# Reordering the front of a fused two-layer kernel: norm powers, table load, modulation and one gating product

## The chip, the cores and the metric

The kernel runs on one core of a Trainium2 chip. A core has five engines that run side by side and meet only at semaphores: TensorE (PE, matrix products; PEld is its weight load), VectorE (DVE), ScalarE (ACT), GpSimd (POOL) and SyncE (SP, which here only issues DMAs). The metric is the device time of one execution in microseconds (us). Three runs of the kernel before gave 589.02, 590.26 and 590.35 us, median 590.26 us.

## The reference

Two residual layers work on x of shape 2 x 1024 x 128 (2048 tokens). Each layer has a mixer half and a feed-forward half, and each half has a LayerNorm, a modulation by a condition vector c (scale `ca`, shift `sa`) and a gate `ga`:

```python
mod = (_silu(L0_c) @ L0_wmod).reshape(L0_c.shape[0], 6, 1, -1)
sa, ca, ga, sb, cb, gb = (mod[:, 0], mod[:, 1], mod[:, 2], mod[:, 3], mod[:, 4], mod[:, 5])
h = _layernorm(x, axis=-1) * (1 + ca) + sa
x = x + ga * _L0_attn_ref(h, ...)
h = _layernorm(x, axis=-1) * (1 + cb) + sb
x = x + gb * _L0_ffn_ref(h, ...)
```

The change is in the first half of layer 0, the spiking mixer `_L0_attn_ref`:

```python
r = jax.nn.sigmoid(jnp.einsum('btd,ed->bte', x, W_r) + b_r)
ek = jnp.exp(jnp.einsum('btd,ed->bte', x, W_k) + b_k)
v = jnp.einsum('btd,ed->bte', x, W_v) + b_v
td = jnp.exp(b_td)
g = jnp.exp(global_decay)
def step(carry, inputs):
    sa, sb, mem = carry
    ek_t, v_t, r_t = inputs
    sa = ek_t * v_t + td * sa
    sb = ek_t + td * sb
    wkv = (g * ek_t * v_t + sa) / (g * ek_t + sb + EPS)
    inp_t = r_t * wkv
    reset = spike_fn(mem - THRESH)
    mem = BETA * mem + inp_t - reset * THRESH
    spk = spike_fn(mem - THRESH)
    return ((sa, sb, mem), spk)
```

After it come two layers of windowed attention with rotary positions and a gelu MLP (layer 0's feed-forward half), a complex linear recurrence (layer 1's mixer), and a mixture of a shared and eight routed experts. The change does not touch them.

## The kernel before

Everything is written as one hand-ordered instruction list per engine; no scheduler reorders it. What an engine issues next is what stands next in its function, and an instruction that waits for a semaphore holds back everything behind it on the same engine.

The tokens are cut into NG = 4 groups of 512 (a group is 4 tiles of 128 tokens). For the mixer the work on a group g goes round all engines:

- DVE computes the LayerNorm statistics of the group's four tiles (`mixer_stats(g)`, L837 to L843) and signals `ln_var`. From the third group on, `ln_stats(n)` first waits until `ln_norm` has reached 4*(n-1), that is, until ACT has normalised group n-2, because the two halves of the statistics buffer are reused.
- POOL raises the variance to the power -1/2 and multiplies by the negated mean (`ln_rstd`, L610 and L611), which signals `ln_rstd`.
- ACT normalises token-major (`mixer_norm(g)`, L359, four instructions, signals `ln_norm`). PE transposes the result (`ln_t2`, L1297). ACT applies modulation scale and shift while it copies it out of the accumulator (`mixer_out(g)`, L365, into `hsA`); for group 0 it first waits for `mod_fin`, the modulation vector from PE (L1336) and DVE (L859 to L867). ACT also copies the transposed input (`mixer_x(g)`, L373).
- PE multiplies by the key weights (L1350) and the value weights (L1353). ACT takes the exponential (L394), scales it (L397, signals `ek_ready`) and makes the denominator's first part `gek` (L399).
- DVE multiplies key by value (L883), scans twice (L889 and L891), forms the numerator (L894, signals `num_ready`) and takes the reciprocal (L897) of the denominator, to which POOL added the scan (L662).
- The quotient and the gating by the sigmoid `rsg` are products of 128 x 512 elements. For groups 0 to 2 POOL does them (`quotient` L651, `current` L657); for group 3 DVE does both (L923, L925).

ACT computes the sigmoids after its loop over the groups. It needs a table of coefficients per set of functions; `load_table` is a tiny instruction that pulls the load to a chosen place. At the start POOL also raises e to the decays and to other per-channel vectors (L631 to L643; `sc_ready` tells that those which ACT needs at L397 are there).

When the gated currents of all groups are there, DVE runs the membrane recurrence as PASSES = 4 passes over chunks of 16 steps (L913 and L917, all 64 chunks of a sequence side by side). The fourth pass checks that the states at the chunks' starts no longer change; if they do, a further checked pass runs. Then the spikes are added to x, and the second norm, the attention and all else follow. PE has products of the identity with itself (`warm`, L1329) before and after the modulation, and after it waits for each group's normalised input in turn.

Of the kernel before, what the change touches and what calls it, by code (L numbers as in the profile page):

```python
# [16 lines left out]
P = 128  # L17
# [58 lines left out]
def program(nc, a, out):  # L76
    with ExitStack() as ctx:
# [266 lines left out]
        def _(act):  # L344
# [23 lines left out]
            def mixer_norm(g):  # L368
                ln_norm(ln_no(0, g), xt[:, g * TPG:(g + 1) * TPG, :])

            def mixer_x(g):
                act.wait_ge(s["xT_fill"], g + 1)
                act.activation(x_cm[:, gsl(g)], psT0[:, :], ACT.Copy).then_inc(s["xT_evac"], 1)  # L373

            def load_table(function):

                act.activation(sc[:, 9:10], half[:, 0:1], function).then_inc(s["table"], 1)
# [6 lines left out]

            mixer_norm(0)
            mixer_x(0)
            mixer_norm(1)
            act.wait_ge(s["init"], 2)
            load_table(ACT.Exp)
            mixer_out(0)  # L390
            for g in range(NG):

                act.wait_ge(s["kv_mm"], 2 * g + 1)
                own.one(act.activation(ek[:, gsl(g)], psS[:, g % 2, :], ACT.Exp, bias=vec[:, V_BK:V_BK + 1]))  # L394
                if g == 0:
                    act.wait_ge(s["sc_ready"], 1)
                act.activation(ek[:, gsl(g)], ek[:, gsl(g)], ACT.Identity, bias=0.0, scale=sc[:, 1:2]).then_inc(s["ek_ready"], 1)  # L397
                act.wait_ge(s["ek_ready"], g + 1)
                act.activation(gek[:, gsl(g)], ek[:, gsl(g)], ACT.Identity, bias=sc[:, 3:4], scale=sc[:, 2:3]).then_inc(s["gek_ready"], 1)  # L399
                if g + 1 < NG:  # L400
                    mixer_x(g + 1)
                    mixer_out(g + 1)
                if g + 2 < NG:
                    mixer_norm(g + 2)
# [191 lines left out]
        def _(pool):  # L596
# [32 lines left out]

            pool.wait_ge(s["ld_c"], 32)  # L630
# [6 lines left out]
            ln_rstd(ln_no(0, 0))  # L637
            ln_rstd(ln_no(0, 1))
# [34 lines left out]
            current(2)  # L673

# [155 lines left out]
        def _(dve):  # L830
# [91 lines left out]
            dve.wait_ge(s["num_ready"], NG)  # L922
            own.one(dve.tensor_tensor(ekv[:, c], ekv[:, c], gek[:, c], ALU.mult))  # L923
            dve.wait_ge(s["r_ready"], NG)
            own.one(dve.tensor_tensor(ekv[:, c], ekv[:, c], rsg[:, c], ALU.mult))  # L925
            dve.wait_ge(s["cur_ready"], NG - 1)
# [366 lines left out]
        def _(pe):  # L1293
# [17 lines left out]

            pe.wait_ge(s["ld_c"], 32)
# [27 lines left out]
            warm(6)  # L1340
            modulation(0, psQK[:, 0, :])
            warm(4)

            ln_t2(ln_no(0, 0))
# [466 lines left out]
```

## Time and profile before

| what | value |
| --- | --- |
| median of three runs | 590.26 us (589.02 to 590.35) |
| profiled execution: its time, its span | 588.94 us, 587.0 us |
| busy share PE, DVE, ACT, POOL | 83%, 77%, 59%, 53% |
| mean granted TensorE clock | 0.929 of full speed |
| start of the stage: DVE's first product of key and value | 17.86 us |
| start of the membrane passes | 48.73 us |
| end of the four passes and their check (next DVE work) | 96.90 us |

The profile is of one execution. The span runs from its first to its last instruction; 1.94 us lie around it. The shares of busy time are means over stages with different limits, so they do not tell what bounds the mixer's front, which ends at 48.73 us. For that a reader takes the timelines of that stretch, engine by engine, and asks of each instruction whether its engine was idle before it and what released it. A timeline line is: start, duration, engine, source line, operation, written tile <- read tiles, shapes, count of merged instructions, and in brackets the idle time before it with its releaser. Instructions of an engine overlap a little, so that the next one can start before start plus duration. An fp32 product is recorded as two instructions.

### The profile page before, as it was taken

The numbers are of one execution on the slowest core, as the hardware profiler recorded it, in microseconds if no ns is written. First come the engines' busy times: TensorE is split into PE (matmuls) and PEld (weight loads), VectorE is DVE, ScalarE is ACT, GpSimd is POOL, SyncE is SP. The second block draws the span as 40 slices with busy tenths as digits, with TensorE's granted clock in tenths as the row PEclk, the third lists the DMA queues.
The fourth block names the chain that finished last, engine by engine and source line by source line (L and its number), as shares of the span: only waits on it lengthen the run. The fifth ranks groups of instructions, "written<-read, shape, count | busy, mean of one in ns | idle before, by whom it ended". The sixth has DMA issues, their size and how long they took to land. (4 is left out here: it accounts for less than half of the span.)

```text
span 587.0 us, 11694 instructions
## 1 busy us (share of the span) xinstructions
PE 488.2 (83%) x3996; PEld 310.8 (53%) x3996; DVE 452.3 (77%) x1201; ACT 348.0 (59%) x1000; POOL 308.5 (53%) x248
## 2 busy tenths in 40 slices
PE   4741004579999999899989999999899999999996
PEld 4411002336777776644347777776644445657774
DVE  5799998779899996646698999996454687457775
ACT  4870000638999998743369999997746535532332
POOL 6650000478888888855878888887001266120000
PEclk9795556689999999999999999999999999999999
DMA  8300000201111111200021111111000000000100
GB/s 302 129 2 0 1 1 1 72 19 28 39 37 39 37 39 37 73 2 1 0 73 39 37 38 38 39 38 35 13 0 2 0 1 1 1 0 5 30 22 18
DMA packets 14192, 18.87 MB, mean 32 GB/s; under 512 B 2186, under 2 KB 8628, under 8 KB 14004
## 3 DMA queue, kind: packets, MB, share of 16 engines
q1 hardware_dynamic: 13844, 18.04, 11.1%
q8 instruction: 32, 0.52, 0.4%
q14 instruction: 28, 0.23, 0.1%
q10 hardware_dynamic: 288, 0.08, 0.1%
HBM read 8.94 MB, written 1.05 MB: 17 GB/s over the span
## 5 line engine op out<-in xcount | busy, mean ns | idle before, releaser
L485 ACT ACTIVATE prob<-psS,nmx 128x128 f32<-128x128 f32 x256 | 89.9, 377 | 21.8 <-DVE nmx L1045 21.8
L610 POOL TENSOR_TENSOR rst<-mv,half 128x4 f32<-128x4 f32 x24 | 25.7, 1069 | 135.0 <-DVE mv L843 124.2
L749 POOL TENSOR_TENSOR rn<-ssq,half 128x16 f32<-128x16 f32 x32 | 93.2, 2911 | 4.3 <-DVE ssq L1031 1.3
L741 POOL TENSOR_TENSOR ra<-ra,rb 128x512 f32<-128x512 f32 x64 | 80.1, 1273 | 3.1 <-DVE rb L1013 3.1
L1371 PE MATMUL psQK<-wqkv,hsA 128*128 128x512 f32 x128 | 64.2, 627 | 2.2 <-ACT z L365 2.2
L359 ACT ACTIVATE lnx<-psT,nmr,rst 128x128 f32<-128x128 f32 x48 | 18.0, 457 | 78.1 <-POOL nmr L611 78.1
L485 ACT ACTIVATION_READ_ACCUMULATOR prob<-psS,nmx 128x1 f32 x256 | 55.5, 217 | 0.0
L757 POOL TENSOR_TENSOR qkn<-ra,rn 128x512 f32<-128x512 f32 x32 | 33.3, 1042 | 28.7 <-DVE qkn L1039 28.7
L1010 DVE TENSOR_TENSOR ra<-psQK,rope 128x512 f32<-128x512 f32 x64 | 43.9, 686 | 5.6 <-PE psQK L1371 5.1
L1013 DVE TENSOR_TENSOR rb<-psQK,rope 128x512 f32<-128x512 f32 x64 | 43.6, 681 | 0.0
L1045 DVE TENSOR_REDUCE nmx<-psS 128x4 f32<-128x512 f32 x64 | 41.1, 683 | 3.1 <-PE psS L1455 3.1
L1297 PEld LDWEIGHTS psT<-ident,qkn 128*128 128x128 f32 x256 | 30.0, 142 | 24.3 <-issue 15.3
L592 ACT ACTIVATE gel<-psQK 128x512 f32<-128x512 f32 x32 | 19.1, 597 | 39.7 <-PE psQK L1655 39.7
L1024 DVE TENSOR_REDUCE ssq<-sq 128x8 f32<-128x512 f32 x64 | 40.9, 676 | 0.2
L1377 PE MATMUL psO<-masks,identb 128*128 128x512 bf16 x12 | 4.5, 557 | 43.8 <-DVE vAB L917 43.8
L1297 PE MATMUL psT<-ident,qkn 128*128 128x128 f32 x256 | 34.5, 276 | 5.8 <-DVE qkn L1039 4.4
L459 ACT ACTIVATE pT<-psT 128x512 f32<-128x512 f32 x64 | 36.5, 656 | 3.0 <-PE psT L1297 3.0
L1473 PE MATMUL psO<-vAB,pT 128*64 128x64 f32 x1024 | 36.9, 225 | 1.6 <-ACT pT L459 1.6
L1297 PEld LDWEIGHTS psT<-ident,prob 128*128 128x128 f32 x256 | 29.7, 140 | 16.0 <-issue 14.0
L1473 PEld LDWEIGHTS psO<-vAB,pT 128*64 128x64 f32 x1024 | 32.4, 138 | 7.7 <-ACT pT L459 5.8
L1409 PE MATMUL psO<-wqkv,hsA 128*128 128x512 f32 x64 | 35.8, 642 | 0.0
L1039 DVE TENSOR_TENSOR qkn<-ra,rn 128x512 f32<-128x512 f32 x32 | 22.1, 691 | 17.7 <-POOL rn L749 17.3
(231 smaller groups left out, 1200.8 us busy)
## 6 DMA issues: line engine op xcount, KB each, us to landing
vAB<-vAB SPq DMA_DIRECT2D x62, 128.0 KB, 2.2
wqkv<-in_wqkv SPq DMA_DIRECT2D x2, 768.0 KB, 7.4
big<-in_x SPq DMA_DIRECT2D x4, 256.0 KB, 4.6
ropeb<-in_rope SPq DMA_DIRECT2D x1, 1024.0 KB, 6.5
big<-in_ew SPq DMA_DIRECT2D x2, 512.0 KB, 4.3
out<-big SPq DMA_DIRECT2D x4, 256.0 KB, 2.3
wmod<-in_wmod SPq DMA_DIRECT2D x2, 384.0 KB, 5.8
w<-in_w SPq DMA_DIRECT2D x2, 341.0 KB
```

Source lines behind the costliest of these rows:

```text
L459: act.activation(pT[:, 4 * hb:4 * hb + 4, :], four((psT0, psT1)[hb]), ACT.Copy).then_inc(s["pT_evac"], 1)
L485: act.activation(prob[:, k, :], psS[:, hb, c * P:(c + 1) * P], ACT.Exp, bias=nmx[:, k:k + 1], accum_out=sums[:, n % 2, k:k + 1]).then_inc( ...
L741: pool.tensor_tensor(o, o, rb[:, r], ALU.add).then_inc(s["sum_" + name], 1)
L749: pool.tensor_tensor(rn[:, :], ssq[:, :], half[:, :], ALU.pow).then_inc(s["rn_ready"], 1)
L1010: dve.tensor_tensor(heads(o), heads(psQK[:, part, :]), rope[:, at8, 2 * part, :].unsqueeze(1).to_broadcast([P, H, DH]), ALU.mult).then_inc ...
L1013: dve.tensor_tensor(rb[:, r].rearrange("p (h a d) -> p h a d", h=H, a=2), psQK[:, part, :].rearrange("p (h a d) -> p h a d", h=H, a=2)[:, ...
L1024: dve.tensor_reduce(ssq[:, 8 * part:8 * part + 8], heads(sq[:, part * INNER:(part + 1) * INNER]), AX.X, ALU.add).then_inc(s["ssq_" + name], 1)
L1045: dve.tensor_reduce(nmx[:, 4 * hb:4 * hb + 4], psS[:, hb, :].rearrange("p (h k) -> p h k", h=4), AX.X, ALU.max, negate=True).then_inc(s["n ...
L1297: i = pe.transpose(dst[:, k * P:(k + 1) * P], src(k), ident[:, :])
L1371: mm(psQK[:, part, :], hsA[:, tile(i)], wqkv[:, part * INNER:(part + 1) * INNER], start=True, stop=True).then_inc(s[name + "_mm"], 1)
L1409: mm(psO[:, 1, :], hsA[:, tile(i)], wqkv[:, 2 * INNER:3 * INNER], start=True, stop=True).then_inc(s["v_fill"], 1)
L1473: j = mm(psO[64 * w:64 * w + 64, 0, h * DH:(h + 1) * DH], pT[:, slot(h), 64 * w:64 * w + 64], (vA, vB)[w][:, u, h * DH:(h + 1) * DH], star ...
```

## The change

Five things move or are added, all in the mixer:

1. POOL raises the first two groups' variances (`ln_rstd` of groups 0 and 1) before the decays instead of after them.
2. ACT loads the table for Exp right after the silu of the condition, before the first norm; it waits for the first of POOL's two memsets only.
3. ACT's norm of group 1 moves from before `mixer_out(0)` to behind group 0's three key instructions; in the same way each norm of group g+1 now stands directly ahead of the copies of group g+1 instead of one group earlier. 
4. PE runs seven 128 x 128 products on zeros (the cleared `kT2`) ahead of its first wait for an input, does the modulation directly behind the first transposes, then three products of the identity, the transposes of the normalised group 0, and four more products of the identity.
5. The gating product of group 3 goes from DVE (L925) to POOL, on the numerator before the quotient: POOL waits for `num_ready` and `r_ready` of all groups and signals `cur_ready`; DVE then has one product left ahead of the passes.

```diff
--- before.py
+++ after.py
@@ -382,11 +382,10 @@
                 b = bof(g)
                 ln_out(ln_no(0, g), hsA[:, gsl(g)], mod[:, 0, CA, b:b + 1], mod[:, 0, SA, b:b + 1])
 
+            act.wait_ge(s["init"], 1)
+            load_table(ACT.Exp)
             mixer_norm(0)
             mixer_x(0)
-            mixer_norm(1)
-            act.wait_ge(s["init"], 2)
-            load_table(ACT.Exp)
             mixer_out(0)
             for g in range(NG):
 
@@ -398,10 +397,9 @@
                 act.wait_ge(s["ek_ready"], g + 1)
                 act.activation(gek[:, gsl(g)], ek[:, gsl(g)], ACT.Identity, bias=sc[:, 3:4], scale=sc[:, 2:3]).then_inc(s["gek_ready"], 1)
                 if g + 1 < NG:
+                    mixer_norm(g + 1)
                     mixer_x(g + 1)
                     mixer_out(g + 1)
-                if g + 2 < NG:
-                    mixer_norm(g + 2)
             for g in range(NG):
                 act.wait_ge(s["r_mm"], g + 1)
                 own.one(act.activation(rsg[:, gsl(g)], psQK[:, g % 2, :], ACT.Sigmoid, bias=vec[:, V_BR:V_BR + 1]))
@@ -627,6 +625,8 @@
 
 
 
+            ln_rstd(ln_no(0, 0))
+            ln_rstd(ln_no(0, 1))
             pool.wait_ge(s["ld_c"], 32)
             own.one(pool.memset(fr[:, 0:1], float(np.e)))
             own.did(pool.tensor_tensor(sc[:, 0:1], fr[:, 0:1], vec[:, V_BTD:V_BTD + 1], ALU.pow))
@@ -634,8 +634,6 @@
             own.one(pool.tensor_scalar(fr[:, 1:2], vec[:, V_BTD:V_BTD + 1], 0.0, -T / 2, ALU.max, ALU.mult))
             own.one(pool.tensor_tensor(sc[:, 1:2], fr[:, 0:1], fr[:, 1:2], ALU.pow))
             pool.tensor_scalar(sc[:, 3:4], sc[:, 1:2], 1e-6, 0.0, ALU.mult, ALU.add).then_inc(s["sc_ready"], 1)
-            ln_rstd(ln_no(0, 0))
-            ln_rstd(ln_no(0, 1))
             for dst, src in ((4, V_NU), (5, V_TH), (6, V_GAM)):
                 own.did(pool.tensor_tensor(sc[:, dst:dst + 1], fr[:, 0:1], vec[:, src:src + 1], ALU.pow))
             own.sync()
@@ -671,6 +669,9 @@
                     current(1)
                     quotient(2)
             current(2)
+            pool.wait_ge(s["num_ready"], NG)
+            pool.wait_ge(s["r_ready"], NG)
+            pool.tensor_tensor(ekv[:, gsl(3)], ekv[:, gsl(3)], rsg[:, gsl(3)], ALU.mult).then_inc(s["cur_ready"], 1)
 
             C1 = 1.0 / (2 * np.pi)
             CH = float(np.round(C1 * 4096 * 4) / (4096 * 4))
@@ -919,11 +920,8 @@
 
 
             dve.wait_ge(s["rcp_ready"], NG)
-            dve.wait_ge(s["num_ready"], NG)
+            dve.wait_ge(s["cur_ready"], NG)
             own.one(dve.tensor_tensor(ekv[:, c], ekv[:, c], gek[:, c], ALU.mult))
-            dve.wait_ge(s["r_ready"], NG)
-            own.one(dve.tensor_tensor(ekv[:, c], ekv[:, c], rsg[:, c], ALU.mult))
-            dve.wait_ge(s["cur_ready"], NG - 1)
             for _ in range(PASSES - 1):
                 membrane_pass(both)
             for st in both:
@@ -1309,6 +1307,10 @@
                 four(out_bank(n), lambda k: lnx[:, n % 2, k, :]).then_inc(s["ln_t2"], 1)
 
 
+            pe.wait_ge(s["init"], 2)
+            nought = kT2[:, 0, 0:2, :]
+            for _ in range(7):
+                mm(psO[:, 0, 0:P], nought, nought, start=True, stop=True)
             pe.wait_ge(s["ld_c"], 32)
 
             def mixer_turn(g):
@@ -1337,11 +1339,10 @@
                            silc[:, 2 * k:2 * k + 2], start=True, stop=True)
                 i.then_inc(s["mod_mm"], 1)
 
-            warm(6)
             modulation(0, psQK[:, 0, :])
+            warm(3)
+            ln_t2(ln_no(0, 0))
             warm(4)
-
-            ln_t2(ln_no(0, 0))
             pe.wait_ge(s["ld_wr"], 16)
             for g in range(NG):
                 pe.wait_ge(s["ln_out"], ln_no(0, g) + 1)
```

On ACT, from the silu of the condition to the second group's copies; before:

```order
L350 ACTIVATE silc<-vec 128x4 [waits ld_c]
L359 ACTIVATE lnx<-big,nmr,rst 128x128 [waits ln_rstd]
L359 ACTIVATE lnx<-big,nmr,rst 128x128 x3
L373 ACTIVATE x_cm<-psT 128x512 [waits xT_fill]
L359 ACTIVATE lnx<-big,nmr,rst 128x128 [waits ln_rstd]
L359 ACTIVATE lnx<-big,nmr,rst 128x128 x3
L377 ACT_TABLE_LOAD
L377 ACTIVATE sc<-half 128x1 [waits init]
L365 ACTIVATE hsA<-psT,mod 128x512 [waits ln_t2,mod_fin]
L394 ACTIVATE big<-psS,vec 128x512 [waits kv_mm]
L397 ACTIVATE big<-big,sc 128x512 [waits sc_ready,act_own]
L399 ACTIVATE big<-big,sc 128x512 [waits ek_ready]
```

and now:

```order
L350 ACTIVATE silc<-vec 128x4 [waits ld_c]
L377 ACT_TABLE_LOAD
L377 ACTIVATE sc<-half 128x1 [waits init]
L359 ACTIVATE lnx<-big,nmr,rst 128x128 [waits ln_rstd]
L359 ACTIVATE lnx<-big,nmr,rst 128x128 x3
L373 ACTIVATE x_cm<-psT 128x512 [waits xT_fill]
L365 ACTIVATE hsA<-psT,mod 128x512 [waits ln_t2,mod_fin]
L393 ACTIVATE big<-psS,vec 128x512 [waits kv_mm]
L396 ACTIVATE big<-big,sc 128x512 [waits sc_ready,act_own]
L398 ACTIVATE big<-big,sc 128x512 [waits ek_ready]
L359 ACTIVATE lnx<-big,nmr,rst 128x128 [waits ln_rstd]
L359 ACTIVATE lnx<-big,nmr,rst 128x128 x3
```

The Exp table now comes second, and the norm of group 1 (the second pair of `lnx` rows) stands behind the three rows on `psS` and `big` of group 0.

On POOL, from its memsets to the end of the first norms' and the decays' powers; before:

```order
L631 MEMSET fr 128x1 [waits ld_c,init]
L632 ISA
L632 TENSOR_TENSOR sc<-fr,vec 128x1 [waits pool_own]
L633 TENSOR_TENSOR sc<-fr,vec 128x1
L634 TENSOR_SCALAR fr<-vec 128x1
L635 TENSOR_TENSOR sc<-fr 128x1 [waits pool_own]
L636 TENSOR_SCALAR sc<-sc 128x1 [waits pool_own]
L610 TENSOR_TENSOR rst<-mv,half 128x4 [waits ln_var]
L611 TENSOR_TENSOR nmr<-nmean,rst 128x4 [waits pool_own]
L610 TENSOR_TENSOR rst<-mv,half 128x4 [waits ln_var]
L611 TENSOR_TENSOR nmr<-nmean,rst 128x4 [waits pool_own]
```

and now:

```order
L608 TENSOR_TENSOR rst<-mv,half 128x4 [waits ln_var,init]
L609 TENSOR_TENSOR nmr<-nmean,rst 128x4 [waits pool_own]
L608 TENSOR_TENSOR rst<-mv,half 128x4 [waits ln_var]
L609 TENSOR_TENSOR nmr<-nmean,rst 128x4 [waits pool_own]
L631 MEMSET fr 128x1 [waits ld_c]
L632 TENSOR_TENSOR sc<-fr,vec 128x1 [waits pool_own]
L633 TENSOR_TENSOR sc<-fr,vec 128x1
L634 TENSOR_SCALAR fr<-vec 128x1
L635 TENSOR_TENSOR sc<-fr 128x1 [waits pool_own]
L636 TENSOR_SCALAR sc<-sc 128x1 [waits pool_own]
```

The two pairs `rst`, `nmr` went ahead of the six instructions from `fr` to `sc`.

On DVE, from the start of the fourth group's statistics to the first product of key and value, the order is the same in both; in the changed kernel it is:

```order
L838 BN_STATS st<-big 128x6 [waits ln_norm,ld_x3]
L838 BN_STATS st<-big 128x6 x3
L841 BN_AGGR mv<-st 128x2 [waits dve]
L841 BN_AGGR mv<-st 128x2 x3
L843 TENSOR_SCALAR nmean<-mv 128x4 [waits dve]
L844 TENSOR_SCALAR mv<-mv 128x4
L884 SCALAR_TENSOR_TENSOR psO<-psO,vec,big 128x512 [waits ek_ready,kv_mm]
L890 SCALAR_TENSOR_TENSOR big<-sc,big 128x512 [waits ekv_ready]
```

The statistics of the fourth group (the row with `ln_norm, ld_x3`) stand ahead of the first product of key and value (the row with `ek_ready,kv_mm`) as before. What moved is the work on ACT that raises `ln_norm` to the awaited value of 8, the norm of group 1.

On DVE, from the last reciprocal to the first step of the passes; before:

```order
L897 RECIPROCAL big<-big 128x512 [waits den_ready]
L907 MEMSET vst 128x64
L923 TENSOR_TENSOR big<-big 128x512 [waits num_ready,rcp_ready]
L925 TENSOR_TENSOR big<-big 128x512 [waits r_ready,dve]
L913 SCALAR_TENSOR_TENSOR vst<-vAB,big 128x64 [waits dve,cur_ready]
L913 SCALAR_TENSOR_TENSOR vst<-vAB,big 128x64 [waits dve_b]
```

and now:

```order
L898 RECIPROCAL big<-big 128x512 [waits den_ready]
L908 MEMSET vst 128x64
L924 TENSOR_TENSOR big<-big 128x512 [waits cur_ready,rcp_ready]
L914 SCALAR_TENSOR_TENSOR vst<-vAB,big 128x64 [waits dve]
L914 SCALAR_TENSOR_TENSOR vst<-vAB,big 128x64 [waits dve_b]
```

One product has gone, and the wait for `cur_ready` stands on the one that remains.

## Rows read from the trace of the kernel before

**Rows 1.** Waits of DVE between 17.5 and 48.7 us: total, times, longest.

```profile
DVE psO L883 <- PE psO L1353: 3.7, 1, 3.7
```

**Rows 2.** Timeline of DVE, first 18 us: start, duration, line, operation, shapes, [idle before].

```profile
5.69 0.16 DVE L843 TENSOR_SCALAR mv<-mv 128x4 f32<-128x4 f32 x1
...
7.54 0.19 DVE L843 TENSOR_SCALAR mv<-mv 128x4 f32<-128x4 f32 x1
10.10 0.17 DVE L859 COPY mod<-psQK 128x12 f32<-128x12 f32 x1 [2.36 <-PE psQK L1336]
...
11.12 0.87 DVE L837 BATCH_NORM_STATS2 st<-big 128x6 f32<-128x128 f32 x4
...
12.62 0.87 DVE L837 BATCH_NORM_STATS2 st<-big 128x6 f32<-128x128 f32 x4
...
17.86 0.76 DVE L883 SCALAR_TENSOR_TENSOR psO<-psO,vec,big 128x512 f32<-128x512 f32 x1 [3.67 <-PE psO L1353]
```

**Rows 3.** Timeline of POOL, first 9 us.

```profile
4.99 0.10 POOL L631 MEMSET fr<- 128x1 f32 x1 [3.28 <-DMA vec<-in_vec]
...
7.52 1.02 POOL L610 TENSOR_TENSOR rst<-mv,half 128x4 f32<-128x4 f32 x1
8.62 0.20 POOL L611 TENSOR_TENSOR nmr<-nmean,rst 128x4 f32<-128x4 f32 x1
```

**Rows 4.** Timeline of ACT, first 24 us.

```profile
4.90 0.21 ACT L350 ACTIVATE silc<-vec 128x4 f32<-128x4 f32 x1 [1.97 <-DMA vec<-in_vec]
8.85 1.65 ACT L359 ACTIVATE lnx<-big,nmr,rst 128x128 f32<-128x128 f32 x4 [3.74 <-POOL nmr L611]
...
12.53 1.28 ACT L377 ACT_TABLE_LOAD   x1
...
13.94 0.76 ACT L365 ACTIVATE hsA<-psT,mod 128x512 f32<-128x512 f32 x1
16.15 0.69 ACT L394 ACTIVATE big<-psS,vec 128x512 f32<-128x512 f32 x1 [1.45 <-PE psS L1350]
...
21.61 0.67 ACT L394 ACTIVATE big<-psS,vec 128x512 f32<-128x512 f32 x1
...
23.79 0.57 ACT L373 ACTIVATE x_cm<-psT 128x512 f32<-128x512 f32 x1
```

**Rows 5.** Timeline of PE, first 32 us.

```profile
5.83 2.77 PE L1329 MATMUL psO<-ident 128*128 128x128 f32 x12
8.39 1.60 PE L1336 MATMUL psQK<-silc,wmod 128*128 128x2 f32 x12
9.85 1.14 PE L1329 MATMUL psO<-ident 128*128 128x128 f32 x8
10.82 0.60 PE L1297 MATMUL psT<-ident,lnx 128*128 128x128 f32 x4
14.84 1.27 PE L1350 MATMUL psS<-hsA,wrkv 128*128 128x512 f32 x2 [3.42 <-ACT hsA L365]
...
30.49 1.12 PE L1350 MATMUL psS<-hsA,wrkv 128*128 128x512 f32 x2 [0.87 <-ACT hsA L365]
```

**Rows 6.** DMA issues between 1.1 and 1.75 us: size, us to landing.

```profile
wmod<-in_wmod SPq DMA_DIRECT2D x1, 384.0 KB, 4.0
```

**Rows 7.** Timeline of DVE, 43 to 49 us.

```profile
43.80 3.34 DVE L897 RECIPROCAL big<-big 128x512 f32<-128x512 f32 x1
...
47.18 0.69 DVE L923 TENSOR_TENSOR big<-big 128x512 f32<-128x512 f32 x1
47.90 0.69 DVE L925 TENSOR_TENSOR big<-big 128x512 f32<-128x512 f32 x1
48.73 0.44 DVE L913 SCALAR_TENSOR_TENSOR vst<-vAB,big 128x64 f32<-128x64 f32 x2
```

**Rows 8.** Timeline of POOL, 43 to 45 us.

```profile
43.29 1.27 POOL L657 TENSOR_TENSOR big<-big 128x512 f32<-128x512 f32 x1
```

**Rows 9.** Timeline of DVE, end of the fourth pass.

```profile
93.21 0.37 DVE L940 TENSOR_TENSOR cend<-cend,vAB 128x128 f32<-128x128 f32 x1
```

## The prediction

> **What bounds the kernel now.** I read the waits of DVE from its first product of key and value to the passes first. There is a single wait, the one before that first product [rows 1]; from 17.86 us [rows 2] to the last reciprocal's end DVE has no idle time, and the passes that begin at 48.73 us [rows 7] are DVE's too. So the end of the mixer is the moment of DVE's first product of key and value plus a gapless stretch of 30.87 us. Only two things can make the mixer shorter: an earlier start of that product, or less work in the stretch. Everything after the passes waits for their spikes, so what is won at 48.73 us is won at the end, and what is won on ACT, PE or POOL alone is not.
>
> Next I read the timelines of the front to see what the start hangs on. DVE finishes group 0's statistics at 5.85 us [rows 2], but POOL is at the decays from 4.99 us and takes up the first norm's power at 7.52 us [rows 3]. ACT norms group 0 from 8.85, norms group 1 behind it, loads the Exp table from 12.53 to 13.81 and only then makes `hsA` at 13.94 us [rows 4]. The key product follows at 14.84 us [rows 5], the exponential at 16.15 us [rows 4], DVE at 17.86 us [rows 2]. PE had the transposes of group 0's norm done at 11.42 us [rows 5], so the norm of group 1 and the table load are what stood in the way.
>
> **The sum's base.** All steps are made against the profiled execution (588.94 us, span 587.0 us, 1.94 us around it). It is 1.32 us below the median of the three runs shown, and I carry the difference over to that median, 590.26 us.
>
> **POOL's powers first.** ln_var of group 0 is there at 5.85 us; POOL is idle since 1.71 us (4.99 less 3.28 [rows 3]). It starts at about 5.92 us. From the start of the power to ACT's norm the trace has 7.52 to 8.85 us, 1.33 us [rows 3, 4], so ACT can norm group 0 at 7.25 us instead of 8.85 us. The norm lasts 1.65 us [rows 4] and ends at 8.90 us. What is late next on POOL: the second power waits for group 1's statistics (7.73 us [rows 2]) and pushes the decays to about 9.05 us (1.25 us per norm, from 7.52 to the end of the `nmr` at 8.62 us and on [rows 3]). They take 2.53 us (4.99 to 7.52 us [rows 3]), so ACT's key scale has what it needs at 11.6 us. It asks for it at about 12.4 us (below): 0.8 us of cover. Cost nothing, up to 0.5 us if group 1's input came late.
>
> **Table load early.** It is 1.28 us plus a tiny activation (12.53 to 13.94 us [rows 4]). Behind the silu, which ends at 5.11 us [rows 4], it runs to 6.5 us, while ACT would be waiting for the norm until 7.25 us. It is hidden, with 0.7 us to spare.
>
> The Trainium skill (ScalarE: Activation LUTs, What ACT_TABLE_LOAD costs) says that a switch costs about 1.28 us for the load and another 1.38 us of draining, 2.66 us in all. By that page ACT would be free only at about 7.9 us, the norm would come 0.65 us later than I take it, and the sum below would be 0.8 us instead of 1.45 us. The trace shows the load's 1.28 us and `hsA` 0.13 us behind it, with the tiny activation between [rows 4], and no drain; I go by the trace.
>
> **Zeros and modulation.** At PE's first pace a 128 x 128 product takes 0.427 us (six in 5.83 to 8.39 us [rows 5]); the seven on zeros start near 1.8 us and are done at 4.8 us, before the inputs are there. They cost nothing where they stand; 0.1 to 0.2 us too much would still be covered, since DVE is not ready for the modulation before 7.73 us. The second group of products of the identity ran at 0.121 us a record (eight from 9.85 to 10.82 us) against 0.213 us before 8.39 us [rows 5]: PE had come from the lower of its two clock levels (1.2 GHz) to the upper (2.4 GHz) while it worked without a gap. With the zeros PE is at work before its first inputs are there, so I take the upper level for the modulation, and the lower one as the bound. The modulation's weights landed 4.0 us after an issue between 1.1 and 1.75 us [rows 6], at 5.7 us at the latest, so its six products can run at 5.85 us and take 1.46 us (8.39 to 9.85 us [rows 5]); at the slow pace 2.6 us. DVE takes them at 7.75 us, behind group 1's statistics, for 1.02 us (10.10 to 11.12 us [rows 2]): the vector is ready at 8.8 us, at the slow pace at 9.5 us. PE transposes the normed group 0 from 8.95 to 9.55 us (0.60 us [rows 5]). So `hsA` starts at 9.6 us, 4.3 us earlier than before. The four identity products behind the transposes (about 1.0 us) end at 10.5 us, just when `hsA` is delivered.
>
> **What DVE gets of it.** `hsA` to key product is 0.90 us (13.94 to 14.84 us [rows 4, 5]), the product 1.12 us at full pace [rows 5] and ACT is 0.04 us behind its end. The exponential starts at 11.7 us, 4.45 us earlier. But DVE's queue holds the fourth group's statistics ahead of the first product, and these wait for ACT's norm of group 1. That norm was done at 12.52 us before (the statistics start at 12.62 us [rows 2]). Now it stands behind the exponential, the scale and `gek` of group 0: these three take 2.18 us (21.61 to 23.79 us [rows 4]), the norm 1.65 us, the signal 0.10 us, the statistics 1.50 us (11.12 to 12.62 us [rows 2]). In sum 5.43 us after the exponential's start: DVE's first product of key and value begins at 11.7 + 5.43 = 17.13 us. The front gives 17.86 - 17.13 = 0.73 us, not 4.4 us; the rest turns into a new wait of DVE of about 5 us for the norm of group 1. The bounds: with the modulation at the slow pace `hsA` starts at 9.95 us and 0.4 us is left; with everything at its best 0.9 us.
>
> Later groups: from norm to norm ACT and PE now need 1.65 + 0.65 + 0.90 + 1.16 + 2.18 = 6.5 us, and DVE needs (47.18 - 17.86)/4 = 7.33 us a group [rows 2, 7]. Group 1's scaled key is ready at about 19.7 us, DVE asks for it near 24.2 us. Moving the later norms costs nothing, and the sigmoids come some tenths earlier.
>
> **Gating on POOL.** DVE loses one product and its wait: L925 starts at 47.90, L923 at 47.18 us, so 0.72 us [rows 7]. POOL has the third group's gating from 43.29 to 44.56 us [rows 8]; the numerator of group 3 is there by 43.88 us and the sigmoids before that, so the new product runs at about 44.5 to 45.8 us, while the reciprocal runs until 47.14 us [rows 7]. The wait for `cur_ready` is over 1.3 us before DVE comes to it. Reciprocals had POOL's products beside them already (43.80 with 43.29 us [rows 7, 8]), at 3.34 us. So the gain is 0.72 us; if the reciprocal did stretch for the added product the gain could go down to about 0.1 us, and nothing else can add to it.
>
> **Sum.** 0.73 + 0.72 = 1.45 us. Profiled execution 587.5 us; beside the median shown, 588.8 us.
>
> **The rivals.**
>
> A: the sum above, 588.8 us.
>
> B: the front gives about nothing, because the key product of group 0 still meets the slow clock (1.12 us more) or the early gaps of PE let the clock fall again. DVE starts at about 17.9 to 18.2 us and only the gating's 0.72 us is left, or less: 589.5 us. For it speaks that PE idles from 10.5 us in short pieces only but did lose its pace in the front before.
>
> C: by the skill's page on the table load, as said: 0.8 us, 589.5 us. Its mechanism here would be a norm of group 0 that starts at 7.9 us.
>
> D: the whole head start reaches DVE: it starts at 11.7 + 1.7 = 13.4 us (16.15 to 17.86 us was 1.71 us [rows 2, 4]), for 4.45 + 0.72 = 5.2 us, 585.1 us. Against it stands the order of DVE's queue, which would have to be wrong.
>
> E, the other side, slower: products on zeros and small gaps leave PE at 1.2 GHz throughout the front. At the slow pace (0.213 us a record [rows 5]) the modulation ends at 8.4 us, three identity products at 9.7 us, the transposes near 10.8 us, four more identity products at 12.2 us, and the key product, now behind them, takes 2.24 us: exponential at 14.5 us, DVE at 14.5 + 5.43 = 19.9 us. That is 2.07 us later, less 0.72 us: 1.35 us slower, 591.6 us. It turns from a gain into a loss where DVE's first product comes after 17.86 + 0.72 = 18.58 us. Against it: even without the zeros PE works nearly without a gap from its first transposes on, as it did before, and the pace rose there before the modulation was through.
>
> F: the new order of the two products changes the last bit of some currents of group 3, and the fourth pass finds a changed state. One more pass is (93.21 - 48.73)/4 = 11.1 us [rows 7, 9] and its check comes on top: 600 us or more. The change of a last bit seldom moves a threshold, and the passes have converged before.
>
> **How the numbers follow.** A 0.68, B 0.14, C 0.04, D 0.04, E 0.08, F 0.02. What a measurement of this kernel can tell from no change is about 0.3%, 1.77 us. A's 1.45 us (0.25%) lies just inside, and medians of three scatter by half a microsecond and more, so of A I count 0.42 as faster: 0.29, with D 0.04 and a little of B and C 0.03 it is 0.36. Slower: F 0.02, a third of E 0.03, scatter 0.02, in all 0.07. The rest, 0.57, is within 0.3%. The range goes from 586.9 us (the best front, 0.9 us, with the lower runs of the scatter) to 590.8 us (half of E's way); it leaves out D, F and most of E.
>
> **What would show it.** In the changed profile: ACT's first norm near 7.25 us, `hsA` near 9.6 us, the exponential near 11.7 us; a wait of DVE of about 5 us before the fourth group's statistics, released by ACT's norm; DVE's first product of key and value at 17.1 us; the passes at 47.3 us; no wait of DVE on POOL ahead of them. The prediction is wrong if DVE starts that product before 16.5 or after 18 us, if the passes start other than 1.2 to 1.7 us earlier, or if the time after the passes changes its length.

## The result and the profile after

The changed kernel takes 606.88 us (median of 4 runs, 605.86 to 607.49) against 589.64 us before (588.74 to 590.35): ratio 1.0291, 95% interval 1.0273 to 1.031. It is 17.2 us slower. The forecast was 588.8 us. The profiled execution has a span of 605.0 us against 587.0 us, 18.0 us more, and every microsecond of it can be found on VectorE. An execution can fall into a slower state with a lower granted TensorE clock; one execution of e8 below did (639.82 us at 0.807), and it is left out of the median and the ratio.

VectorE's timeline after (the same columns as in [rows 2]):

```profile
18.08 0.87 DVE L838 BATCH_NORM_STATS2 st<-big 128x6 f32<-128x128 f32 x4 [6.91 <-ACT lnx L359]
...
19.55 0.76 DVE L884 SCALAR_TENSOR_TENSOR psO<-psO,vec,big 128x512 f32<-128x512 f32 x1
...
47.02 3.35 DVE L898 RECIPROCAL big<-big 128x512 f32<-128x512 f32 x1 [1.58 <-POOL big L660]
...
50.41 0.69 DVE L924 TENSOR_TENSOR big<-big 128x512 f32<-128x512 f32 x1
51.21 0.44 DVE L914 SCALAR_TENSOR_TENSOR vst<-vAB,big 128x64 f32<-128x64 f32 x2
...
95.71 0.37 DVE L938 TENSOR_TENSOR cend<-cend,vAB 128x128 f32<-128x128 f32 x1
...
98.90 0.19 DVE L954 MEMSET vst<- 128x64 f32 x2 [1.07 <-issue]
...
110.44 0.37 DVE L938 TENSOR_TENSOR cend<-cend,vAB 128x128 f32<-128x128 f32 x1
...
113.85 0.49 DVE L967 TENSOR_SCALAR big<-vAB,mod 128x512 f32<-128x512 f32 x1 [1.29 <-issue]
```

and the first spikes in the kernel before, which [rows 9] does not reach:

```profile
96.90 0.49 DVE L969 TENSOR_SCALAR big<-vAB,mod 128x512 f32<-128x512 f32 x1 [1.57 <-issue]
```

Four things are to be seen, in order of time.

1. The first product of key and value (L884) starts at 19.55 us, where it started at 17.86 us [rows 2]: 1.69 us later. The statistics ahead of it (18.08 us) had waited for ScalarE.
2. The last reciprocal (L898) starts after 1.58 us of idle time, released by GpSimd's denominator sum (L660). Before, VectorE had no idle time there at all [rows 1, 7]. One product (0.72 us) is gone between it and the passes, which begin at 51.21 us instead of 48.73 us: 2.48 us later, and 1.69 + 1.58 - 0.72 = 2.55 us.
3. The comparison of the states (L938) is there twice. The first one at 95.71 us comes 44.50 us after the passes' begin, as before (93.21 less 48.73 us is 44.48 us [rows 7, 9]). Then the memset of the branch follows (98.90 us), a whole pass and a second comparison at 110.44 us. From the passes' begin to the first spikes it is 113.85 - 51.21 = 62.64 us; before it was 96.90 - 48.73 = 48.17 us. This is an extra pass with its test, at 14.47 us.
4. From the first spikes to the end of the span it is 605.0 - 113.85 = 491.15 us; before, 587.0 - 96.90 = 490.10 us. 1.05 us more.

In sum 2.48 + 14.47 + 1.05 = 18.0 us.

The waits of VectorE between 8 and 50 us after (total, times, longest) name the two releasers in the front:

```profile
DVE st L838 <- ACT lnx L359: 6.9, 1, 6.9
DVE big L898 <- POOL big L660: 1.6, 1, 1.6
```

TensorE after, the front, the first work behind the passes and the first product for attention:

```profile
1.77 3.36 PE L1313 MATMUL psO<-kT 128*128 128x128 f32 x14 [1.77 <-POOL kT L597]
...
5.92 2.56 PE L1338 MATMUL psQK<-silc,wmod 128*128 128x2 f32 x12
8.34 1.63 PE L1331 MATMUL psO<-ident 128*128 128x128 f32 x6
9.77 1.06 PE L1295 MATMUL psT<-ident,lnx 128*128 128x128 f32 x4
10.62 1.92 PE L1331 MATMUL psO<-ident 128*128 128x128 f32 x8
12.32 1.79 PE L1351 MATMUL psS<-hsA,wrkv 128*128 128x512 f32 x2
...
115.12 1.11 PE L1295 MATMUL psT<-ident,x_cm 128*128 128x128 f32 x4 [18.01 <-DVE x_cm L970]
...
126.12 3.62 PE L1372 MATMUL psQK<-wqkv,hsA 128*128 128x512 f32 x4
```

The records of the zeros, of the modulation (12 in 8.34 - 5.92 = 2.42 us, 0.20 us each) and of the identity products (six from 8.34 to 9.77 us, 0.24 us each) all have the pace that [rows 5] shows ahead of 8.39 us; I read from the pace that TensorE is at its lower clock level (1.2 GHz) until the key product at 12.32 us, which lasts 1.79 us. The granted clock itself cannot be used here: that column reads 1.00 in this trace until 20 us, and in every trace until its first fall, also where the records are slow. Where it does read 0.50 on the same products, in the run e10 below from 9.9 to 11.6 us, eight identity records take 1.71 us, 0.21 us each; the eight from 10.62 to 12.32 us here take 1.70 us.

At 126.12 us four records last 3.62 us, at a granted clock of 0.50. The like pieces before:

```profile
98.16 1.11 PE L1297 MATMUL psT<-ident,x_cm 128*128 128x128 f32 x4 [3.12 <-DVE x_cm L972]
...
109.16 2.90 PE L1371 MATMUL psQK<-wqkv,hsA 128*128 128x512 f32 x4
```

ScalarE after:

```profile
7.29 1.65 ACT L359 ACTIVATE lnx<-big,nmr,rst 128x128 f32<-128x128 f32 x4 [0.57 <-POOL nmr L609]
...
10.93 0.78 ACT L365 ACTIVATE hsA<-psT,mod 128x512 f32<-128x512 f32 x1 [1.51 <-PE psT L1295]
14.16 0.69 ACT L393 ACTIVATE big<-psS,vec 128x512 f32<-128x512 f32 x1 [2.45 <-PE psS L1351]
...
16.35 1.63 ACT L359 ACTIVATE lnx<-big,nmr,rst 128x128 f32<-128x128 f32 x4
...
36.03 0.69 ACT L393 ACTIVATE big<-psS,vec 128x512 f32<-128x512 f32 x1 [1.97 <-PE psS L1351]
...
39.63 0.69 ACT L405 ACTIVATE big<-psQK,vec 128x512 f32<-128x512 f32 x1
```

The norm starts at 7.29 us as forecast, the modulated copy at 10.93 us (forecast 9.6 us), the exponential at 14.16 us (11.7 us). The last group's exponential is at 36.03 us and the first sigmoid at 39.63 us. Before, the sigmoids began at 35.25 us:

```profile
31.65 0.69 ACT L394 ACTIVATE big<-psS,vec 128x512 f32<-128x512 f32 x1 [1.22 <-PE psS L1350]
...
35.25 0.69 ACT L407 ACTIVATE big<-psQK,vec 128x512 f32<-128x512 f32 x1
```

GpSimd after:

```profile
41.12 3.42 POOL L655 TENSOR_TENSOR big<-big 128x512 f32<-128x512 f32 x2 [2.45 <-ACT big L406]
44.50 1.26 POOL L649 TENSOR_TENSOR big<-big 128x512 f32<-128x512 f32 x1
45.72 1.26 POOL L660 TENSOR_TENSOR big<-big 128x512 f32<-128x512 f32 x1
...
48.16 1.26 POOL L674 TENSOR_TENSOR big<-big 128x512 f32<-128x512 f32 x1
```

The gatings of groups 0 and 1 (L655) begin at 41.12 us, when the first sigmoids are there; behind them stand a quotient (L649) and only then the denominator sum of group 3 (L660, 45.72 us) for which VectorE waits. The new product (L674, 48.16 us) is over before VectorE's last product at 50.41 us.

### The profile page after: what moved, and what is told of

Same layout as the page of the kernel before. It is cut to its first block and busy times, and to the rows that moved or that the text cites. A ratio compares the mean times of both kernels' runs of the same rounds, so it can differ in the third digit from the quotient of the medians.

```text
span 605.0 us, 11793 instructions
## 1 busy us (share of the span) xinstructions
PE 494.3 (82%) x4004; PEld 314.4 (52%) x4004; DVE 465.0 (77%) x1276; ACT 348.5 (58%) x1000; POOL 311.0 (51%) x249
## 3 DMA queue, kind: packets, MB, share of 16 engines
HBM read 8.94 MB, written 1.05 MB: 17 GB/s over the span
## 5 line engine op out<-in xcount | busy, mean ns | idle before, releaser
L1372 PE MATMUL psQK<-wqkv,hsA 128*128 128x512 f32 x128 | 66.9, 650 | 2.7 <-ACT z L365 2.7
L914 DVE SCALAR_TENSOR_TENSOR vst<-vAB,big 128x64 f32<-128x64 f32 x160 | 35.7, 273 | 0.3
```

Of the source, the lines that this page charges most:

```text
L1372: mm(psQK[:, part, :], hsA[:, tile(i)], wqkv[:, part * INNER:(part + 1) * INNER], start=True, stop=True).then_inc(s[name + "_mm"], 1)
```

## The experiments

Each run has runs of the kernel before on the same chip beside it; "before" in a line is the median of those. Each profile is of one execution.

**The order of the two products.** Three runs take the last part of the change by itself.

```diff
# e1: the changed kernel, part 5 undone
-            pool.wait_ge(s["num_ready"], NG)
-            pool.wait_ge(s["r_ready"], NG)
-            pool.tensor_tensor(ekv[:, gsl(3)], ekv[:, gsl(3)], rsg[:, gsl(3)], ALU.mult)...
-            dve.wait_ge(s["cur_ready"], NG)
+            dve.wait_ge(s["num_ready"], NG)
             own.one(dve.tensor_tensor(ekv[:, c], ekv[:, c], gek[:, c], ALU.mult))
+            dve.wait_ge(s["r_ready"], NG)
+            own.one(dve.tensor_tensor(ekv[:, c], ekv[:, c], rsg[:, c], ALU.mult))
+            dve.wait_ge(s["cur_ready"], NG - 1)
```

> The changed kernel with one part undone: group 3's quotient and then its gating are both on VectorE again, in the old order. Theory R (rounding): the new order of the two products (gating before the quotient) changes low bits of group 3's currents, the fourth pass finds a changed state and one more pass of about 14.4 us, test of the states included, runs. Then this kernel has no extra pass and takes about 606.9 - 14.4 + 0.7 = 593.2 us. Rival T (table): the extra pass comes from the first norm being computed under another ScalarE table; then the extra pass stays and the time is about 607.6 us.

Measured 590.44 us (before 590.09 us; ratio 1.0019, 1.0003 to 1.0035). The states are compared once, at 95.00 us: there is no extra pass. The run is 2.8 us better than expected. In the profiled executions 1.4 us of that is the front (its passes begin at 50.50 us, those of the changed kernel at 51.21 us with one product of 0.72 us less) and 0.7 us the time behind the passes (490.41 against 491.15 us).

e2 is the kernel before with part 5 of the change alone.

> The kernel before with only the gating of group 3 moved to GpSimd and ahead of the quotient. Theory R: an extra pass, about 589.6 - 0.7 + 14.4 = 603.3 us. Rival T: no extra pass, about 588.9 us.

Measured 603.40 us (before 590.09 us; ratio 1.0239, 1.0222 to 1.0256), with the extra pass (comparisons at 92.16 and 106.90 us); the passes begin at 47.64 us.

```diff
# e3: the kernel before
             dve.wait_ge(s["num_ready"], NG)
-            own.one(dve.tensor_tensor(ekv[:, c], ekv[:, c], gek[:, c], ALU.mult))
             dve.wait_ge(s["r_ready"], NG)
             own.one(dve.tensor_tensor(ekv[:, c], ekv[:, c], rsg[:, c], ALU.mult))
+            own.one(dve.tensor_tensor(ekv[:, c], ekv[:, c], gek[:, c], ALU.mult))
```

> The kernel before with group 3's two products both left on VectorE, only their order exchanged (numerator times sigmoid, then times reciprocal). Theory R: the order alone brings the extra pass, about 604.0 us. Rival G (it is GpSimd's product, not the order, that gives other bits): no extra pass, 589.6 us.

Measured 604.44 us (before 590.09 us; ratio 1.0254, 1.0237 to 1.0271). The instructions that read or write the compared states show the comparison twice (count, durations in ns, first and last start in us):

```profile
L940 DVE TENSOR_TENSOR cend<-cend,vAB x2: 374/376/378, 93.2 to 107.9; 128x128 f32<-128x128 f32 x2
```

Same engine, same instructions, another order of two multiplications: the extra pass is there. So neither GpSimd nor ScalarE's table makes it. What is left is the rounding: in fp32 (n * r) * q and (n * q) * r can differ in the last bit. No run read the bits themselves.

**Is it that order, or luck?** e8 exchanges the same two products for group 2, on GpSimd, in the kernel before.

```diff
# e8: the kernel before, on GpSimd
-                    quotient(2)
-            current(2)
...
+                    pool.tensor_tensor(ekv[:, gsl(2)], ekv[:, gsl(2)], rsg[:, gsl(2)], ALU.mult).then_inc(s["quot_ready"], 1)
...
+            pool.tensor_tensor(ekv[:, gsl(2)], ekv[:, gsl(2)], gek[:, gsl(2)], ALU.mult).then_inc(s["cur_ready"], 1)
```

> The kernel before with the two products exchanged in order for group 2 instead of group 3 (both on GpSimd). Theory L (which last bits converge in four passes is luck of the data): the outcome is open for this group, about 590 us without an extra pass or 604.5 us with it; seen together with group 3. Rival S (gating before the quotient always costs the extra pass, as a property of that order): 604.5 us for sure. Only 590 us tells them apart.

Measured 589.67 us (seven executions; before 589.66 us; ratio 1.0, 0.9986 to 1.0013), and one comparison only:

```profile
L944 DVE TENSOR_TENSOR cend<-cend,vAB x1: 374/374/374, 92.7 to 92.7; 128x128 f32<-128x128 f32 x1
```

The order as such does not cost a pass: for group 3 it does, for group 2 it does not. So it hangs on which last bits these data get. No run had other inputs, and only these two exchanges were tried.

**How near the kernel before is to it.** e12 sets PASSES to 3.

> The kernel before with three passes instead of four, the third one tested. Theory L (the states are settled only just in time, by luck of the last bits): the third pass still changes a state, one tested pass is added, and the price of the repeat over a planned pass shows alone: 14.5 - 11.1 = 3.4 us slower, about 593.1 us. Rival: the states are settled after two passes, then it is 11.1 us faster, 578.6 us, and the kernel has a whole pass in reserve.

Measured 594.07 us (before 589.62 us; ratio 1.007, 1.0053 to 1.0086):

```profile
L940 DVE TENSOR_TENSOR cend<-cend,vAB x2: 375/376/377, 82.8 to 97.5; 128x128 f32<-128x128 f32 x2
```

With three passes the third one still changes a state, so the kernel before uses all four and has no pass in reserve. The repeat costs 4.45 us more than a planned pass; expected were 3.4 us. From the passes' begin to the first spikes it is 3.53 us more than before (51.70 against 48.17 us), as expected; the profiled execution has another 1.7 us behind the passes (491.82 against 490.10 us).

**What is left without the extra pass.** e4 is the changed kernel without the branch; it leaves out every further pass, so its states for group 3 may be unsettled.

```diff
# e4
             changed = checked_pass(both)
-            with dve.If(changed != 0):
-                ...
```

> The changed kernel without the branch behind the fourth pass: it leaves out the further passes whether the states still change or not, so group 3's membrane may be unconverged. It gives the part of the loss that is not the extra pass: the passes begin 2.5 us later than before, so about 589.6 + 2.5 = 592.1 us, less what the branch itself costs. If it stays above 594 us, time is lost behind the passes as well.

Measured 589.08 us (before 590.09 us; ratio 0.9995, 0.9978 to 1.0012), 3 us better than expected. The spans of the profiled executions, 588.4 us here and 605.0 us for the changed kernel, lie 16.6 us apart:

- 14.47 us are the extra pass;
- 1.36 us lie behind the passes (491.15 against 489.79 us);
- 0.58 us is what the branch costs even when it is not taken, since e4 has none (47.59 us from the passes' begin to the first spikes against 48.17 us before);
- 0.19 us is the front. The passes begin at 51.02 us here. VectorE's first product came 1.0 us earlier (18.53 us), but its last reciprocal then waited longer, 2.81 us against 1.58 us, with a fourth scan that was 0.4 us shorter.

The medians lie 17.8 us apart, 1.2 us more, because e4's profiled execution (590.33 us) was 1.25 us above its median.

**The front.** e1's profile shows the front without the extra pass. VectorE:

```profile
15.75 0.87 DVE L835 BATCH_NORM_STATS2 st<-big 128x6 f32<-128x128 f32 x4 [5.12 <-ACT lnx L359]
...
17.22 0.75 DVE L881 SCALAR_TENSOR_TENSOR psO<-psO,vec,big 128x512 f32<-128x512 f32 x1
...
45.55 3.35 DVE L895 RECIPROCAL big<-big 128x512 f32<-128x512 f32 x1 [2.82 <-POOL big L660]
```

TensorE:

```profile
5.77 1.74 PE L1338 MATMUL psQK<-silc,wmod 128*128 128x2 f32 x12
7.38 0.91 PE L1331 MATMUL psO<-ident 128*128 128x128 f32 x6
...
17.23 2.08 PE L1351 MATMUL psS<-hsA,wrkv 128*128 128x512 f32 x2 [0.87 <-ACT hsA L365]
```

ScalarE:

```profile
11.82 0.69 ACT L393 ACTIVATE big<-psS,vec 128x512 f32<-128x512 f32 x1 [1.28 <-PE psS L1351]
...
19.34 0.69 ACT L393 ACTIVATE big<-psS,vec 128x512 f32<-128x512 f32 x1 [2.17 <-PE psS L1351]
```

Here TensorE (second block) came to its upper level during the modulation (six identity products in 0.91 us). The exponential is at 11.82 us and VectorE's first product at 17.22 us; the forecast had 11.7 and 17.13 us. But the time from one group's exponential to the next is 7.5 us, since TensorE idles in between and makes the second key product at the lower level (2.08 us, at a granted clock of 0.50 from 17 to 19 us), and VectorE then waits 2.82 us for the last denominator sum.

e9 is the kernel before with part 3 alone, the norms' order.

```diff
# e9: the kernel before, on ScalarE
             mixer_x(0)
-            mixer_norm(1)
...
                 if g + 1 < NG:
+                    mixer_norm(g + 1)
                     mixer_x(g + 1)
                     mixer_out(g + 1)
-                if g + 2 < NG:
-                    mixer_norm(g + 2)
```

> The kernel before with one part of the change alone: ScalarE's norm of each group g+1 stands behind group g's three key instructions. Theory N: VectorE's fourth statistics wait for the norm of group 1, so its first product of key and value comes near 20 us (2.2 us late), and the late sigmoids make the last reciprocal wait for GpSimd by 1.2 to 2.8 us: in all 3.4 to 5 us slower, about 594 us. Rival (the norms' order is harmless, as the prediction had it for the later groups, and only the start counts): 2.2 us slower, 591.8 us.

Measured 593.54 us (before 589.62 us; ratio 1.0066, 1.0051 to 1.0081): 3.9 us slower. VectorE's waits between 8 and 60 us:

```profile
DVE st L835 <- ACT lnx L359: 5.4, 1, 5.4
DVE big L895 <- POOL big L660: 2.8, 1, 2.8
```

Both waits of the changed kernel are there with that part alone. The passes begin at 53.02 us, 4.29 us late: 1.89 us from the first product (19.75 us) and 2.82 us for the denominator, less 0.4 us. The 0.4 us are VectorE's fourth scan, 1.29 us long instead of 1.80 us. In the kernel before GpSimd was already at a product (from 39.58 us) when that scan began at 40.13 us; here GpSimd began 0.45 us behind the scan, and its two gatings took 3.13 us instead of 2.50 us.

e7 keeps the norms' new order and takes the gatings of groups 0 and 1 out of the way on GpSimd.

```diff
# e7: e1, on GpSimd
                 elif g == 2:
                     quotient(1)
-                    current(0)
-                    current(1)
                     quotient(2)
+            current(0)
+            current(1)
             current(2)
```

> The run with the gating back on VectorE and the norms in the change's new order, and in GpSimd's queue the gatings of groups 0 and 1 moved behind group 3's denominator sum. Theory N: the 2.8 us wait of the last reciprocal goes, about 590.4 - 2.8 = 587.7 us. Rival: the reciprocal then waits for something else (numerator, scan) and the time stays at 590 us; or the gatings, now late, hold the passes, 588.5 us.

Measured 589.27 us (before 589.66 us; ratio 1.0, 0.9986 to 1.0014). The wait for the denominator is gone:

```profile
DVE st L835 <- ACT lnx L359: 6.7, 2, 6.4
```

From VectorE's first product to the passes it is 30.88 us, as in the kernel before (30.87 us) and 2.40 us less than in e1 (33.28 us). The time is not to be told from that of the kernel before and 1.6 us above the expectation: in the profiled execution VectorE started 1.2 us later than in e1's (18.46 us).

e5 is e1 with the norms' old order too, so parts 1, 2 and 4 of the change.

> As the run with the gating back on VectorE, and also ScalarE's norms back in their old places (norm of group 1 ahead of group 0's copy, norm of group g+2 at the end of group g's turn). What is left of the change: powers first, table load and modulation forward, products on zeros. Theory N (the norms' new order is what costs the front: VectorE waits 5.1 us for group 1's norm, and late sigmoids hold GpSimd's queue so that the last reciprocal waits 2.8 us): VectorE's first product of key and value comes at about 14.8 us, no wait before the last reciprocal, 3.0 us faster than the kernel before, about 587.0 us. Rival P (the front hangs on TensorE's pace whatever the norms do): 589 to 590.5 us.

Measured 585.77 us (5 runs, 585.48 to 586.12; before 589.66 us; ratio 0.9935, 0.9921 to 0.9948). VectorE's waits between 8 and 60 us:

```profile
DVE psO L883 <- ACT big L397: 2.3, 1, 2.3
DVE st L837 <- ACT lnx L359: 0.8, 2, 0.5
```

Its first product is at 14.93 us, 2.93 us earlier than before, nothing waits for the denominator, and the passes begin at 45.82 us, 2.91 us earlier. This version beats both kernels.

e6 is e5 without the products on zeros.

> The run with gating and norms back, and without the seven products on zeros. If the zeros bring TensorE to its upper clock level earlier (theory Z), the modulation runs at the lower one here and the time is 0.4 to 1.0 us above the run with zeros. If they do nothing (rival), the two are equal within 0.2 us, about 587.0 us.

Measured 586.81 us (before 589.66 us; ratio 0.9949, 0.9935 to 0.9963), 1.0 us above e5; the two intervals overlap a little. TensorE with the zeros (e5):

```profile
5.78 1.46 PE L1340 MATMUL psQK<-silc,wmod 128*128 128x2 f32 x12
7.10 0.91 PE L1333 MATMUL psO<-ident 128*128 128x128 f32 x6
```

and without them (e6):

```profile
5.50 2.69 PE L1336 MATMUL psQK<-silc,wmod 128*128 128x2 f32 x12
8.05 1.63 PE L1329 MATMUL psO<-ident 128*128 128x128 f32 x6
```

With the zeros the modulation goes in 1.46 us, without them in 2.69 us, and the six identity records behind in 0.91 against 1.63 us. That fits what the zeros were meant for, but these are two single executions, and the last section shows that the moment of the rise differs between executions of the same front.

e10 puts ScalarE's norm of group 1 behind `mixer_out(0)` in e5; e11 also leaves out the four identity products behind the transposes.

> The fastest version so far (gating and norms back, 585.8 us), with ScalarE's norm of group 1 moved behind group 0's modulated copy and ahead of its exponential. While TensorE makes the key product, ScalarE norms group 1. Theory N: the copy is 1.1 us earlier, VectorE's first product 0.5 to 1.2 us earlier, about 584.9 us. Rival P (the key product stands behind four identity products and runs at TensorE's lower clock level, so it is not earlier): 585.8 us.

> The same as the run with norm 1 behind the copy, and without the four identity products ahead of the key product. If they only stand in the way, the key product starts up to 0.9 us earlier and the time is 0.3 to 0.9 us lower, about 584.3 us. If they keep TensorE's clock at its upper level, leaving them out costs some tenths of a microsecond.

Measured 586.27 us (ratio 0.9934, 0.9921 to 0.9947) and 586.63 us (0.9949, 0.9933 to 0.9965), before 589.62 us. Neither beats e5. In e10 VectorE's first product is at 14.48 us, 0.45 us earlier, but its first reciprocal (19.00 us) then waits for GpSimd's denominator sum of group 0, and the passes begin at 46.41 us, 0.59 us later than in e5:

```profile
DVE st L837 <- ACT lnx L359: 2.2, 2, 2.0
DVE big L897 <- POOL big L662: 0.6, 1, 0.6
```

## Why the prediction was wrong

**The step that failed most** is the judgement under F: "The change of a last bit seldom moves a threshold, and the passes have converged before." The mechanism was named, its place was right, and its price was put at 11.1 us and a test, 600 us or more; the chance of 0.02 was wrong. Both halves of the sentence fail. e12 shows that the kernel before needed all four passes: the third still changed a state. And the test is not one of thresholds: in the printed kernel (L940) it compares the fp32 states for inequality, so a last bit that has not settled is enough, whether a spike moves or not. Which of the two it was in the changed kernel no run shows. e3 shows that the order of the products alone brings the extra pass, e8 that the same exchange for another group does not. That it hit this change is luck of the data, and nothing in the trace of before could tell it. But the fixed number of 4 passes with a test behind it stood in the kernel, and its reserve could have been measured by one run. 14.47 of the 18.0 us are this.

The three signs that the prediction named against itself all came: VectorE's first product after 18 us (19.55 us), the passes outside 1.2 to 1.7 us earlier (2.48 us later), and another length behind the passes (1.05 us more).

**Gating on GpSimd**, 0.72 us less on VectorE: right. e2's passes begin at 47.64 us and e3's at 48.66 us; with the difference of their first products (17.51 and 17.78 us) taken off, 0.75 us.

**Powers first and table load**: right. The norm came at 7.29 us (7.25 us forecast) in the changed kernel. The early load took 1.28 us, from 5.22 us, and the tiny activation started 0.01 us behind its end, so the table load had no drain behind it; C did not happen.

**Zeros and modulation**: the term had two ends, and the changed kernel's profile fell beyond the worse one. The bound of 9.95 us had only the modulation at the slow pace. The identity products and the transposes behind it ran at the lower level too, in front of each other, and the copy started at 10.93 us, as E had it: exponential 14.16 us (E: 14.5 us), first product 19.55 us (E: 19.9 us). The other profiles with zeros (e1, e4, e5, e7, e10, e11) reached the upper level before the modulation was through. So E's mechanism is one that happened in one of seven profiled executions. Whether the changed kernel meets it more often than the others stays open. For it speaks that e4's median with the extra pass (14.47 us), the branch (0.58 us) and the longer time behind the passes (1.36 us) comes to 605.5 us, and its four runs (605.86 to 607.49 us) are all above that.

**What VectorE gets of it**: the new wait for the norm of group 1 was forecast at about 5 us and was 6.9 us in the changed kernel and 5.1 us in e1, where the first product came within 0.1 us of the forecast. From the exponential to the first product the forecast had 5.43 us; it was 5.39 us and 5.40 us. The step was right.

**Later groups: failed.** "Moving the later norms costs nothing, and the sigmoids come some tenths earlier." A group was to take 6.5 us from exponential to exponential, so that the last exponential would come near 31.3 us. In e1 a group took 7.7 us (11.82 to 35.02 us), in the changed kernel 7.3 us from a later start (14.16 to 36.03 us). I had taken TensorE at its upper level. With the norm now in the chain TensorE idles 1.4 to 2.6 us ahead of each transpose of a normed group, and of the six key products behind such a stretch in these two profiles five took 1.88 to 2.08 us and one 1.13 us, where the full pace is 1.12 us. And I had looked only at who waits for the key, not at the sigmoids at the end of ScalarE's list: GpSimd waits for them with the last denominator sum queued behind. That made 1.58 us in the changed kernel, 2.8 us in e1, e4 and e9. e7, which only reorders GpSimd's list, removes the wait; e5, which puts the norms back, removes this wait and most of the other one and gains what the front had to give: 3.9 us in the medians, 2.9 us at the passes' begin, instead of my 0.73 us.

Without the extra pass the total would have looked right: e4 took 589.08 us where 588.8 us were forecast. That is luck. Its passes began 2.29 us later than before, not 1.45 us earlier, and it lacks the branch.

**After the passes**: 1.05 us more, not forecast. TensorE's last products during the passes stand ahead of the test of the fourth pass; with an extra pass TensorE idles 17.4 to 18.0 us before its next work instead of 3.1 us. Three of the four profiles with an extra pass (the changed kernel, e3, e12) have 491.2 to 491.8 us behind the passes, and their first product for attention lasts 3.62 us, at a granted clock of 0.50. The fourth (e2) has 490.1 us, and there that product lasts 2.73 us. The profiles without an extra pass have 489.8 to 490.5 us. So the loss goes with a slower clock in the first work behind the passes, which a long idle stretch does not always bring. No run isolated it.

## What to carry to other kernels

Where a kernel tests a floating-point state for exact equality and repeats work if it fails, the order of two multiplications ahead of the test can be part of the performance: look for the branch, ask how many rounds it has in reserve (one run with one round less tells), and time a reordered product by itself. Where an instruction moves inside one engine's list, follow every later result of that engine to the queue that takes it, and read what stands behind the waiting instruction there. A move that brings the first group's copy forward (a norm out of its way) can be wrong for the loop; test the parts of a combined change one by one, as three good parts (0.65% together) were hidden here behind two bad ones.

## What the runs showed of the hardware

TensorE's pace in the first 13 us differs between executions of nearly the same instructions. With the zeros, six of seven profiled executions were at the upper level before the first identity products behind the modulation (0.15 us a record, e1 and e5), one was at the lower until 12.3 us (0.24 us a record). Of the seven profiled executions without them the level rose between about 8 and 9 us in five and not before 12 us in two (e6, e8). The Trainium skill (TensorE: Matmul & The Clock Gate, What's actually happening) says that the number of slow products at the start varies from run to run of the same kernel. The traces agree with it, as far as single executions of nearly the same front can: in the kernel before and in e8, whose instructions are the same up to there, the modulation took 1.46 and 2.42 us. With the changed kernel's order of the norms, the rise moved VectorE's first product between 17.22 and 19.55 us.
